# A new order of the calls on all five engines of an attention and mixture-of-experts kernel

## What is computed

```python
xn = _layernorm(x)                       # x: (2, 512, 512)
x = x + attn(xn) + ffn(xn)

def attn(x):                             # 32 query heads, 8 KV heads, 128 numbers each
    q, k, v = x @ Wq.T, x @ Wk.T, x @ Wv.T
    q = q * cos + rotate_half(q) * sin   # k likewise
    scores = einsum('bkgtd,bksd->bkgts', q, k) / sqrt(128)   # causal, float32
    out = einsum('bkgts,bksd->bkgtd', softmax(scores), v)
    return einsum('bto,ho->bth', out, Wo)

def ffn(xt):                             # 16 experts of 512 x 128, two for each row, by group
    y = sum over experts of gate * ((silu(xt @ w1 + b1) * (xt @ w2 + b2)) @ w3 + b3)
    return y + (silu(xt @ sw1 + sb1) * (xt @ sw2 + sb2)) @ sw3 + sb3
```

## Time and profile before

| | before |
|---|---|
| median of 3 executions | 911.94 us (909.39 to 912.68) |
| the profiled execution | 912.02 us |
| span of its profile, first to last instruction | 910.3 us |
| mean granted TensorE clock | 0.992 |
| busy TensorE | 870.0 us, 4,638 matmuls |
| busy VectorE, POOL, ScalarE | 705.4, 515.9, 432.0 us |
| busy weight loads of TensorE (beside the matmuls) | 728.9 us |

### The profile page before, as it was taken

One profiled execution on the slowest core, in us unless ns is written; L12 is line 12 of the kernel. 1 busy time (PEld: TensorE's weight loads), 2 busy tenths in 40 slices (PEclk: granted clock), 3 DMA queues, 4 the chain that ended last, 5 costly groups with the idle time before them and its releaser, 6 DMA issues.

```text
span 910.3 us, 16509 instructions
## 1 busy us (share of the span) xinstructions
PE 870.0 (96%) x4638; PEld 728.9 (80%) x4638; DVE 705.4 (77%) x1551; ACT 432.0 (47%) x1074; POOL 515.9 (57%) x614
## 2 busy tenths in 40 slices
PE   8999999999899989999899998999899998999987
PEld 7788778888688878888788877888788877888775
DVE  5656778778868797788867798778877798688885
ACT  3512353365454554545444554455445554455442
POOL 5835656445655556655555466555455466554572
PEclk9999999999999999999999999999999999999999
DMA  9935571113422353242522353232623253231252
GB/s 336 325 116 185 184 249 59 47 53 113 154 76 99 94 188 98 90 141 77 187 76 98 86 179 95 101 120 74 202 87 105 86 173 92 84 117 43 87 163 75
DMA packets 71249, 114.11 MB, mean 125 GB/s; under 512 B 6448, under 2 KB 34736, under 8 KB 70960
## 3 DMA queue, kind: packets, MB, share of 16 engines
q1 hardware_dynamic: 68656, 105.32, 36.2%
q0 software_dynamic: 2560, 8.39, 2.8%
HBM read 82.76 MB, written 30.93 MB: 125 GB/s over the span
## 4 chain that ended last, share of the span: by engine, by line
PE 69%; DVE 11%; issue 8%; DMA 7%; POOL 3%; ACT 1%; SPq 1%; DVEq 0%; ACTq 0%; POOLq 0%
PE bank L1994 7%; PE bank L1996 6%; PE bank L1995 6%; DMA w_raw<-w 6%; PE bank L2242 5%; PE bank L2246 5%; PE bank L2243 5%; PE bank L2129 5%; PE bank L2131 5%; PE bank L2130 5%; PE bank L2208 4%; PE bank L2223 3%; PE bank L2226 3%; PE bank L2224 3%; PE bank L2150 1%
## 5 line engine op out<-in xcount | busy, mean ns | idle before, releaser
L658 POOL TENSOR_SCALAR prob<-prob,rsum 128x128 f32<-128x128 f32 (+3 forms) x256 | 145.3, 587 | 187.5 <-DVE rsum L1492 187.4
L890 ACT ACTIVATE prob<-bank,nmax 128x128 f32<-128x128 f32 (+3 forms) x256 | 133.0, 526 | 129.9 <-DVE nmax L1486 127.7
L1486 DVE CUSTOM_DVE_ANT_0 bank<-bank,causal 128x128 f32<-128x128 f32 (+3 forms) x256 | 122.4, 501 | 54.5 <-PE bank L1996 51.7
L1514 DVE TENSOR_TENSOR pT_lo<-bank,pT_hi 128x512 fp32r<-128x512 f32 x160 | 108.1, 683 | 37.4 <-ACT pT_hi L913 36.3
L913 ACT ACTIVATE pT_hi<-bank 128x512 fp32r<-128x512 f32 x160 | 92.8, 595 | 67.2 <-PE bank L2208 37.1
L2242 PE MATMUL bank<-wo_lo,oT_hi 128*128 128x512 f32 x256 | 103.2, 403 | 0.8 <-DVE wo_lo L1532 0.8
L2129 PE MATMUL bank<-xT_hi,wq_lo 128*128 128x512 f32 x256 | 102.3, 400 | 0.6 <-DVE rot L1446 0.6
L2131 PE MATMUL bank<-xT_hi,wq_hi 128*128 128x512 f32 x256 | 102.0, 399 | 0.0
L2130 PE MATMUL bank<-xT_lo,wq_hi 128*128 128x512 f32 x256 | 101.3, 396 | 0.0
L2246 PE MATMUL bank<-wo_hi,oT_lo 128*128 128x512 f32 x256 | 100.9, 394 | 0.0
L2243 PE MATMUL bank<-wo_hi,oT_hi 128*128 128x512 f32 x256 | 100.7, 393 | 0.0
(11 more groups left out here) (225 smaller groups left out, 2215.8 us busy)
## 6 DMA issues: line engine op xcount, KB each, us to landing
w_raw<-w SPq DMA_DIRECT2D x31, 512.0 KB, 3.9
wq_raw<-wq SPq DMA_DIRECT2D x32, 256.0 KB, 6.0
v_all<-v_stage SPq DMA_DIRECT2D x16, 512.0 KB
v<-v_all SPq DMA_DIRECT2D x16, 512.0 KB, 6.1
wo_raw<-wo SPq DMA_DIRECT2D x32, 256.0 KB, 3.2
xg<-x_slots SPq DMA_DIRECT2D x31, 256.0 KB, 3.7
eb<-b SPq DMA_DIRECT2D x31, 256.0 KB, 3.8
w_raw<-w SPq DMA_DIRECT2D x31, 256.0 KB, 2.8
```

The source lines that it names most:

```text
L658: last = nc.gpsimd.tensor_scalar(row, row, rsum[:, stat(b, i, h)], 1.0, ALU.mult, ALU.mult)
L890: last = nc.scalar.activation(prob[n % 2][:, h, 0:P * (i + 1)], bank[S_BANKS[use % 2]][:, 256 * k:256 * k + P * (i + 1)], ACT.Exp, bias=nm ...
L1486: last = nc.vector.tensor_tensor_reduce(s, s, causal[:, TB * P - width:TB * P], -1.0, -MASKED * 3.0, ALU.add, ALU.min, nmax[:, stat(b, i, h)])
```

## The change

The lists of the three kinds of stage get another order on all five engines. No call is added, taken away or changed, and no call goes from one kind of stage to another or from one engine to another; the opening and the functions that are called stay. On VectorE, operations that read two operands in SBUF (such as lo_kT, which reads krot and kT_hi there) stand elsewhere relative to POOL's long subtractions (lo_w12, split_q). On SP the loads come in another order. The diff has some 1,950 lines; its core follows, by engine.

SP, in key_head:

```diff
             def key_head(g):
-                load_wk(g)
                 e1 = load_x(tile_of(g, 1))
                 load_w12(tile_of(g, 1), e1)
+                load_wk(g)
                 load_b12(tile_of(g, 1), e1)
+                load_w3(tile_of(g, 1), e1)
                 load_wo(g, 0)
-                store_y(tile_of(g, 0))
                 load_wo(g, 1)
                 load_wo(g, 2)
+                e2 = load_x(tile_of(g, 2))
+                load_wo(g, 3)
+                store_y(tile_of(g, 0))
                 load_b3(tile_of(g, 1), e1)
-                load_wo(g, 3)
-                load_w3(tile_of(g, 1), e1)
-                e2 = load_x(tile_of(g, 2))
+                load_wq(g, 0)
                 load_b12(tile_of(g, 2), e2)
+                load_wq(g, 1)
                 load_w12(tile_of(g, 2), e2)
-                load_wq(g, 0)
-                load_wq(g, 1)
                 load_wq(g, 2)
+                e3 = load_x(tile_of(g, 3))
+                store_y(tile_of(g, 1))
...
+                load_w3(tile_of(g, 4), e4)
                 store_y(tile_of(g, 3))
-                load_w3(tile_of(g, 4), e4)
                 e5 = load_x(tile_of(g, 5))
                 load_w12(tile_of(g, 5), e5)
-                load_v(g + 1, 0)
+                load_b3(tile_of(g, 4), e4)
                 load_b12(tile_of(g, 5), e5)
-                load_b3(tile_of(g, 4), e4)
+                store_y(tile_of(g, 4))
                 load_w3(tile_of(g, 5), e5)
```

POOL, in key_head:

```diff
             def key_head(g):
                 lo_w12(tile_of(g, 0))
-                lo_w3(tile_of(g, 0))
+                add_k(g, 1)
                 normalise(g, 0, 0)
                 normalise(g, 0, 1)
-                add_k(g, 1)
-                lo_w12(tile_of(g, 1))
+                lo_w3(tile_of(g, 0))
                 split_k(g + 1)
                 add_q(g, 1, 0)
+                lo_w3(tile_of(g, 1))
+                lo_w12(tile_of(g, 1))
                 normalise(g, 0, 2)
                 add_q(g, 1, 1)
-                lo_w3(tile_of(g, 1))
                 add_q(g, 1, 2)
                 lo_w12(tile_of(g, 2))
                 normalise(g, 0, 3)
                 add_q(g, 1, 3)
                 split_q(g + 1, 0)
+                split_q(g + 1, 1)
                 lo_w3(tile_of(g, 2))
+                normalise(g, 1, 0)
                 lo_w12(tile_of(g, 3))
-                split_q(g + 1, 1)
-                split_q(g + 1, 2)
-                normalise(g, 1, 0)
+                lo_w3(tile_of(g, 3))
+                add_k(g + 1, 0)
                 normalise(g, 1, 1)
                 add_q(g + 1, 0, 0)
+                split_q(g + 1, 2)
                 split_q(g + 1, 3)
-                lo_w3(tile_of(g, 3))
                 normalise(g, 1, 2)
+                add_q(g + 1, 0, 1)
                 lo_w12(tile_of(g, 4))
-                add_k(g + 1, 0)
-                add_q(g + 1, 0, 1)
                 add_q(g + 1, 0, 2)
                 lo_w3(tile_of(g, 4))
                 normalise(g, 1, 3)
                 add_q(g + 1, 0, 3)
```

ScalarE, in key_head, from hi_w12(1) on:

```diff
-                hi_w12(tile_of(g, 1))
+                hi_kT(g, 1)
+                expert_tanh(tile_of(g, 0))
                 exps(g, 0, 1, 0)
                 exps(g, 0, 1, 1)
+                hi_pT(g, 0, 0, 0)
                 hi_oT(g - 1, 1, 3)
                 hi_hT(tile_of(g, 0))
                 exps(g, 0, 2, 0)
-                hi_pT(g, 0, 0, 0)
                 exps(g, 0, 2, 1)
+                hi_pT(g, 0, 1, 0)
+                hi_pT(g, 0, 1, 1)
+                hi_xg(tile_of(g, 1))
+                hi_oT(g, 0, 0)
                 exps(g, 0, 2, 2)
                 exps(g, 0, 2, 3)
-                hi_pT(g, 0, 1, 0)
-                hi_xg(tile_of(g, 1))
-                hi_pT(g, 0, 1, 1)
-                hi_wo(g, 0)
-                hi_oT(g, 0, 0)
+                hi_w3(tile_of(g, 1))
+                hi_w12(tile_of(g, 1))
                 hi_q(g, 1, 0)
...
-                hi_w3(tile_of(g, 1))
-                hi_pT(g, 0, 2, 0)
-                hi_w12(tile_of(g, 2))
-                hi_hT(tile_of(g, 1))
                 exps(g, 0, 3, 2)
                 exps(g, 0, 3, 3)
+                hi_wo(g, 3)
+                hi_q(g, 1, 1)
+                expert_tanh(tile_of(g, 1))
+                hi_oT(g, 0, 1)
+                hi_pT(g, 0, 2, 0)
+                hi_hT(tile_of(g, 1))
                 hi_q(g, 1, 2)
-                hi_oT(g, 0, 1)
+                hi_w12(tile_of(g, 2))
                 hi_pT(g, 0, 2, 1)
                 hi_xg(tile_of(g, 2))
                 hi_pT(g, 0, 2, 2)
+                hi_oT(g, 0, 2)
+                exps(g, 1, 0, 0)
+                expert_tanh(tile_of(g, 2))
                 hi_pT(g, 0, 3, 0)
+                last_hi_q(g, 1)
+                hi_pT(g, 0, 3, 1)
+                hi_hT(tile_of(g, 2))
                 hi_w3(tile_of(g, 2))
-                hi_pT(g, 0, 3, 1)
-                expert_tanh(tile_of(g, 2))
-                hi_oT(g, 0, 2)
+                hi_pT(g, 0, 3, 2)
+                hi_pT(g, 0, 3, 3)
                 hi_w12(tile_of(g, 3))
-                hi_hT(tile_of(g, 2))
-                exps(g, 1, 0, 0)
-                hi_pT(g, 0, 3, 2)
-                last_hi_q(g, 1)
                 exps(g, 1, 0, 1)
```

VectorE, in key_head: the new list up to lo_kT(g, 1), and the old one around it:

```diff
+                add_b12(tile_of(g, 0))
+                inverse_sums(g, 0, 0)
+                maxima(g, 0, 1, 0)
+                maxima(g, 0, 1, 1)
+                expert_product(tile_of(g, 0))
+                lo_kT(g, 1)
+                expert_hidden(tile_of(g, 0))
+                inverse_sums(g, 0, 1)
...
-                lo_q(g, 1, 1)
-                turn_q1(g, 1, 2)
-                turn_q2(g, 1, 2)
-                maxima(g, 0, 3, 2)
-                lo_pT(g, 0, 2, 0)
-                lo_hT(tile_of(g, 1))
-                lo_kT(g, 1)
-                maxima(g, 0, 3, 3)
-                add_out(g, 0, 0)
-                add_b3(tile_of(g, 1))
```

TensorE, in key_head, from expert_up(2) on: the new list, then the old one:

```diff
+                expert_up(tile_of(g, 2))
+                transpose_p(g, 0, 3, 0)
+                transpose_p(g, 0, 3, 1)
+                project_k(g + 1, 0, 0)
+                project_k(g + 1, 0, 1)
+                project_k(g + 1, 0, 2)
+                project_k(g + 1, 0, 3)
+                scores(g, 1, 0, 1)
+                transpose_p(g, 0, 3, 2)
+                transpose_p(g, 0, 3, 3)
+                transpose_h(tile_of(g, 2))
+                values(g, 0, 3, 0)
+                values(g, 0, 3, 1)
+                project_q(g + 1, 0, 0, 0)
+                project_q(g + 1, 0, 0, 1)
+                expert_down(tile_of(g, 2))
+                scores(g, 1, 1, 0)
+                project_q(g + 1, 0, 0, 2)
+                project_q(g + 1, 0, 0, 3)
+                values(g, 0, 3, 2)
+                values(g, 0, 3, 3)
+                transpose_p(g, 1, 0, 0)
+                transpose_x(tile_of(g, 3))
+                project_out(g, 0, 2, 0)
+                scores(g, 1, 1, 1)
+                project_out(g, 0, 2, 1)
+                project_out(g, 0, 2, 2)
+                project_out(g, 0, 2, 3)
+                scores(g, 1, 2, 0)
+                scores(g, 1, 2, 1)
+                expert_up(tile_of(g, 3))
+                scores(g, 1, 2, 2)
+                values(g, 1, 0, 0)
+                project_q(g + 1, 0, 1, 0)
+                project_out(g, 0, 3, 0)
...
-                expert_up(tile_of(g, 2))
...
                 values(g, 0, 2, 1)
                 values(g, 0, 2, 2)
                 transpose_p(g, 0, 3, 0)
                 transpose_p(g, 0, 3, 1)
-                project_k(g + 1, 0, 0)
-                scores(g, 1, 0, 0)
-                project_k(g + 1, 0, 1)
-                scores(g, 1, 0, 1)
-                project_k(g + 1, 0, 2)
-                transpose_p(g, 0, 3, 2)
-                transpose_h(tile_of(g, 2))
-                transpose_p(g, 0, 3, 3)
                 project_out(g, 0, 1, 0)
-                values(g, 0, 3, 0)
-                project_k(g + 1, 0, 3)
                 project_out(g, 0, 1, 1)
                 project_out(g, 0, 1, 2)
...
                 values(g, 0, 3, 1)
-                scores(g, 1, 1, 0)
-                project_out(g, 0, 1, 3)
-                project_q(g + 1, 0, 0, 0)
-                expert_down(tile_of(g, 2))
-                scores(g, 1, 1, 1)
-                project_q(g + 1, 0, 0, 1)
-                project_q(g + 1, 0, 0, 2)
...
                 values(g, 0, 3, 2)
                 values(g, 0, 3, 3)
-                transpose_x(tile_of(g, 3))
-                transpose_p(g, 1, 0, 0)
-                project_q(g + 1, 0, 0, 3)
-                scores(g, 1, 2, 0)
-                project_out(g, 0, 2, 0)
                 project_out(g, 0, 2, 1)
-                project_out(g, 0, 2, 2)
-                expert_up(tile_of(g, 3))
-                project_out(g, 0, 2, 3)
-                scores(g, 1, 2, 1)
-                scores(g, 1, 2, 2)
-                project_q(g + 1, 0, 1, 0)
-                project_q(g + 1, 0, 1, 1)
-                project_q(g + 1, 0, 1, 2)
```

(69 more changed lines are left out.)

1147 lines of the change are left out of this document (551 added, 596 removed).

## The result

| | before | after |
|---|---|---|
| median | 910.66 us (907.15 to 912.68, 4 executions) | 874.68 us (874.14 to 875.09, 4 executions) |
| ratio | | 0.961, 95% interval 0.958 to 0.964 |
| span | 910.3 us | 872.4 us |
| start to first matmul of the first middle head | 190.51 us | 187.64 us |
| six middle heads, each | 103.9 us | 99.2 us |

The account below looks back on a forecast made before the run. TensorE's order of calls was taken as the bound. Span 910.3 - 22 (middle heads) - 4.5 (last head) + 1.5 (first head) = 885.3 us, plus 1.7 gives 887 us; own range 879 to 896, wide range 871 to 910.

Parts of the forecast that it names:

- the likeliest case: Whole kernel: the forecast of 887 us, own range 879 to 896, chance 0.52.
- rival A: Whole kernel: nearly all waits go and no new ones come, 870 us; chance 0.14.
- Middle heads, -22: Six middle heads: 34 us of waits and clock dips removed, 12 us of new waits added, net -22 us.
- five places: Places in TensorE's new middle-head order with under 0.5 us to spare, taken at 0.4 us of new wait each.
- Step 1: ScalarE, middle heads: later hi_w12(1) and hi_w12(2) remove waits behind the exponential and lo_hT, 1.4 us a head.
- Step 2: VectorE and POOL, middle heads: moving lo_kT(g, 1) takes 1.9 us from the queue before add_b3(1); hidden-operation wait goes too.
- Step 3: SP, middle heads: loads reordered by a few places, each waiting for a matmul far enough ahead; no separate size.
- First head, +1.5: First head: later lo_v(2) and add_first_q cost +1.5 us, bounds -1.5 and +5.
- Last head, -4.5: Last head: about 8 us to win, less 1 us for lo_oT and 2.5 for the rest; bounds 0 and -8.
- B: Middle heads: five places and meetings with POOL's short operations cost 3.5 us a head, half the gain, 900 us; chance 0.17.
- C: Whole kernel: POOL's short operations hold VectorE up like long ones, so no change, 912 us; chance 0.08.
- D: Middle heads: exps(g, 1, 0, 1) behind hi_w12(3) waits for a late load; 921 us at 14 us load time; chance 0.09.

Follow-up runs that it names:

- kernel 3: Kernel before, with ScalarE's hi_w12(1) moved behind exps(g, 0, 2, 3) and hi_w12(2) behind hi_hT(1) in the middle heads: 892.46 us.
- kernel 4: Kernel before, with only VectorE's lo_kT(g, 1) moved from ahead of add_b3(1) to behind it in the middle heads: 896.90 us.
- kernel 5: Kernel before, with ScalarE's hi_w12(1) and hi_w12(2) later and VectorE's lo_kT(g, 1) behind add_b3(1) in the middle heads: 891.86 us.
- kernel 6: Kernel before, with POOL's subtraction lo_w12 of 128 x 1024 cut into four of 128 x 256, all orders kept: 894.67 us.
- kernel 7: kernel 3 with POOL's split_q(g + 1, 0) also moved behind lo_w12(3) in the middle heads: 885.51 us.
- kernel 9: Changed kernel, with SP's issue of load_w12(3) moved behind load_w3(3), about 10 us later, in the middle heads: 914.62 us.
- kernel 1: Kernel before, with the five new lists of the middle heads alone; first and last head keep their old lists: 882.99 us.
- kernel 11: Changed kernel, VectorE's lo_hT(2) behind turn_k, add_b3(2) ahead of turn_q1; first head: lo_kT(0, 0) ahead of first_lo_q(0), lo_v(2) ahead of count_blocks: 868.98 us.
- kernel 2: Kernel before, with the new lists of the first and last head alone: 902.05 us.
- kernel 8: Changed kernel, with VectorE's lo_hT(2) moved directly behind turn_k(g + 1, 0) in the middle heads: 871.67 us.
- kernel 12: Changed kernel, with POOL's last two normalisations put back behind the gathers in the last head: 880.81 us.
- kernel 10: Changed kernel, with ScalarE's hi_w12(1) put back ahead of exps(g, 0, 1, 0) and hi_w12(2) ahead of hi_hT(1): 890.53 us.

## Why the prediction was right, and where it was off

The sign, the mechanism in the main and the wide range held: 874.7 against 871 to 910. The number of the likeliest case, 887, was 12 us too high, and the measured time lies below that case's own range of 879 to 896, between it and rival A's 870. That the wide range holds it is owed to its having been drawn to take in most of A, which had a chance of 0.14; the case with 0.52 did not come. The spans' difference to the sum, 885.3 - 872.4 = 12.9 us, splits by its terms:

- **Middle heads, -22: measured -28.2.** The removed part was sized right, 34 us. Of the new waits, for which the sum had 12 us, there are 6 x 0.73 us, with 0.16 for each 5.3 us; -34 + 5.3 = -28.7. This term, 0.4 us at each of five places, is the largest miss, 6.2 us. Four of the five places show no wait. At the fifth, expert_down(2), there is one, but behind lo_hT(2) and not behind lo_w3(2). The walk over the queues had left every place above zero, and filling them with the smallest wait of the present kernel had no row behind it.
- **Step 1, ScalarE.** Right in kind, and worth more than was said: 18.1 us (kernel 3). But it does not by itself take away the wait behind lo_hT: 3.5 of 8.0 us stay, behind VectorE's own queue. The prediction held it and step 2 for two causes, and put 1.4 us a head to the first (by its own rows 10.6 us in six heads, 1.8). They are one chain (kernels 4 and 5).
- **Step 2, VectorE and POOL.** lo_kT(g, 1) is free, as said (it moves forward by 37 calls, not 30), and the waits behind add_b3 and the hidden operation are gone. The mechanism is shown by kernels 3, 6 and 7. But the meetings are only moved in part: last_lo_q now takes 1.62 us. VectorE's busy time falls by no more than 13.7 us. It is the place of a meeting that counts.
- **Step 3, SP.** No wait for a load holds TensorE up. Kernel 9 shows that the place of one issue decides the sign.
- **Clock dips.** Gone from the middle heads, as said.
- **First head, +1.5: measured -2.9.** Wrong in sign. 0.6 us of it stands already at the first project_v, 51.17 against 51.80 us, in code that the diff leaves alone. lo_v(2) costs 0.26 us of wait and not 1. add_first_q behind six more scatters costs nothing: scores(g, 0, 0, 0) waits 0.52 us, and for lo_kT(0, 0). Three waits of 0.60 to 0.64 us in the old order, which the prediction had not read, are gone or down to 0.25. Which call removed them was not tried. The 2.9 us themselves are loose: with the old lists the first middle head began at 190.5 to 191.0 us in the traces of the kernel before and kernels 1, 3 and 4, but at 188.9 to 189.0 in those of kernels 5, 6 and 7, where the wait of 0.60 us was absent with nothing moved in the first head. With the new lists, kernel 11 aside, it began at 187.6 to 188.5. Within a group of runs the gain is 3.1 us (kernels 1 to 4) and 1.1 (kernels 5 to 8).
- **Last head, -4.5: measured -6.8.** Right in kind. The 2.5 us that were left for the rest were not needed. Kernel 12 shows that the place of the normalisations alone is worth 6.1 us in the new order.
- **The rivals.** A is nearest: all waits but one went. B (3.5 us a head for waits) and C (no gain, since POOL's short operations block too) did not come. Short ones do block, as last_lo_q and the 0.94 us of lo_kT(g + 1, 0) show, but only the first made TensorE wait, 0.73 us a head. D needs a load later than it is; at about 5 us of delay of the exponential it costs 6.35 us a head, more than the one for one that I gave it, since the clock falls too.

## What to carry to other kernels

In a kernel whose bound engine runs a fixed list, follow each wait back through the queues to the first late thing before counting causes: here one copy that stood too early in ScalarE's queue, waiting for its load, made two kinds of TensorE wait, and repairing both links brought no more than repairing the first. Put a copy that waits for a load behind the short operations that others need, and ask how late the load may be before it blocks what stands behind it. Look for VectorE operations with two SBUF operands beside long POOL instructions just ahead of a link of a chain; move the one, so that it begins first or meets nothing, or cut the other into pieces. Where it begins first by 0.03 us, as in kernel 3, the margin is that small.

## What the runs showed of the hardware

- Between a VectorE subtraction on two SBUF operands and a POOL subtraction, the one that begins first decides. lo_kT behind POOL's start ends 0.54 to 0.56 us behind POOL's end, whether POOL's instruction takes 2.39 us (kernel before), 1.30 (changed kernel) or 0.73 (kernel 6). lo_kT ahead of POOL by 0.03 to 0.39 us takes 0.68 us, and POOL's subtraction takes 2.56 to 2.92 us and not 2.39 (kernel 3).
- The block holds POOL up elsewhere too: beside VectorE's four operations of combine_two, POOL's normalisation of four rows of 384 took 3.73 us and not 2.27 (kernel 12), while VectorE's four took 3.73 us, where such a call takes 3.11 to 3.24 in the changed kernel.
- The price of a wait grows with what follows it. Waits of 3.5 to 3.7 us in kernel 9 were followed by 4 us at a granted clock of 0.50 to 0.69 in each of the six heads, and a head took 6.35 us more. Shorter waits did it in some heads alone: in the kernel before, pairs of 1.12 to 1.17 and 1.69 to 1.75 us, some 4 us apart, were followed by a dip (0.59 to 0.64 over 4 us) in three heads, while the pairs of 1.02 and 1.69, 1.81 and 1.70, and 1.73 and 1.70 us in the other three left the clock at 1.00. So the length of the waits does not tell them apart, and what does is open. In kernel 10 pairs of 0.43 to 1.43 and 0.66 to 0.70 us, 3 us apart, brought none.
- POOL's subtraction of 128 x 1024 in four pieces took 2.82 to 2.88 us where nothing of VectorE got in and 3.27 with lo_kT let in, against 2.39 in one.
